# A fused transformer, minGRU, Runge-Kutta and expert kernel: another order of the fourth head's low parts, the last gates by k block, and most of the last drive's split moved into the first Runge-Kutta round

## What is computed

```
x = x + minGRU(adaLN_transformer(x, cond))        # 16 heads of 128, attention within a sequence; MLP 1024, gelu
x = x + top4_of_16_blocks_ffn(RK4(cond, cond, drive = x))

minGRU:  z = sigmoid(x Wz + bz);  n = g(x Wn + bn);  h_t = (1 - z_t) h_(t-1) + z_t n_t,  h_0 = 0.5
RK4:     per token step four stages of  dq = q - q^3/3 - p + drive + tanh(q) C^T + bias,  dp = 0.08 (q + 0.7 - 0.8 p)
ffn:     h = gelu(q W1^T), the 12 blocks of 64 columns with the smaller router logits set to 0;  y = h W2^T
```

## Time and profile before

| | us |
|---|---|
| median of 3 runs | 519.38 (519.37 to 520.13) |
| the profiled execution | 521.38 |
| its span | 519.5 |
| attention, four passes | to about 243 |
| MLP and gates | about 243 to 330 |
| Runge-Kutta scan | about 330 to 508 |

### The profile page before, as it was taken

How to read it: one execution, slowest core, us unless ns; L and a number is a source line. 1 busy time by engine, 2 the same in 40 slices (tenths; PEclk the granted TensorE clock), 3 DMA queues, 4 the chain that set the end, 5 groups by cost and what they waited for, 6 DMA issues and landing times.

```text
span 519.5 us, 13419 instructions
## 1 busy us (share of the span) xinstructions
PE 449.8 (87%) x4832; PEld 310.7 (60%) x4832; DVE 434.4 (84%) x1698; ACT 314.2 (60%) x872; POOL 48.4 (9%) x77
## 2 busy tenths in 40 slices
PE   2999989999999899997498996589797887888886
PEld 2655675557546665566244442478676776767676
DVE  4969876777776876979978776999999999999994
ACT  1378855786487748775467935464655646555563
POOL 2001320224021211042000000000000000000000
PEclk9899999999999999999789999596979879788899
DMA  8972402200202000000000000000000000000000
GB/s 292 415 305 62 105 4 78 61 21 0 81 21 61 0 1 0 0 1 0 0 1 1 0 1 0 3 2 0 2 1 11 11 0 11 1 11 11 1 10 22
DMA packets 10127, 20.82 MB, mean 40 GB/s; under 512 B 1456, under 2 KB 4720, under 8 KB 9456
## 3 DMA queue, kind: packets, MB, share of 16 engines
q1 hardware_dynamic: 9536, 19.89, 11.4%
q10 hardware_dynamic: 560, 0.60, 0.3%
HBM read 19.40 MB, written 1.08 MB: 39 GB/s over the span
## 4 chain that ended last, share of the span: by engine, by line
DVE 43%; PE 37%; ACT 10%; issue 5%; POOL 2%; DMA 2%; ACTq 0%; DVEq 0%
PE bank L765 33%; DVE base L1567 5%; DVE lin L1659 5%; DVE qs L1573 4%; DVE cub L1561 3%; DVE sq L1555 3%; ACT ptx L567 3%; PE score L765 3%; ACT ao_sb L535 2%; DVE pacc L1669 2%; POOL ptx L471 2%; ACT sraw L560 2%; PE spare L765 2%; DMA vec<-vecs 2%; DVE thlo L1551 1%
## 5 line engine op out<-in xcount | busy, mean ns | idle before, releaser
L765 PE MATMUL bank<-x,pairs_store 128*128 128x512 f16 x384 | 87.2, 384 | 0.0
L765 PE MATMUL score<-th,coup_part 128*128 128x32 f16 x1024 | 48.1, 182 | 19.4 <-ACT th L728 17.3
L765 PEld LDWEIGHTS bank<-x,pairs_store 128*128 128x128 f16 x384 | 37.7, 99 | 43.8 <-issue 2.2
L471 POOL TENSOR_TENSOR ptx<-pt,ptx 32x256 f16<-32x256 f32 x64 | 44.5, 696 | 190.8 <-ACT ptx L567 187.2
L535 ACT ACTIVATE big<-bank,pass_b 128x512 f16<-128x512 f32 x64 | 42.1, 683 | 23.5 <-DVE pass_b L1286 15.8
L728 ACT ACTIVATE th<-qs 128x64 f16<-128x64 f32 x96 | 24.4, 254 | 50.5 <-DVE qs L1573 50.5
L765 PEld LDWEIGHTS score<-th,coup_part 128*128 128x128 f16 x1024 | 36.4, 100 | 30.8 <-ACT th L728 29.3
L1298 DVE SCALAR_TENSOR_TENSOR big<-bank,pass_b,big 128x512 f16<-128x512 f32 x64 | 45.2, 739 | 7.5 <-ACT big L535 7.3
L765 PE MATMUL bank<-pairs_store,ao_sb 128*128 128x256 f16 x384 | 46.1, 273 | 5.2 <-DVE ao_sb L1298 1.9
L765 PEld LDWEIGHTS bank<-pairs_store,ao_sb 128*128 128x128 f16 x384 | 35.8, 98 | 12.7 <-DVE ao_sb L1298 4.3
L765 PE MATMUL bank<-pairs_store,x 128*128 128x512 f16 x192 | 43.4, 379 | 0.0
(11 more groups left out here) (197 smaller groups left out, 1017.9 us busy)
## 6 DMA issues: line engine op xcount, KB each, us to landing
wqk_sb<-wqk SPq DMA_DIRECT2D x16, 256.0 KB, 2.9
wv_sb<-wv SPq DMA_DIRECT2D x4, 512.0 KB, 5.7
wo_sb<-wo SPq DMA_DIRECT2D x4, 512.0 KB, 3.9
f_sb<-ffn_w SPq DMA_DIRECT2D x2, 1024.0 KB, 14.1
ao_sb<-xtok SPq DMA_DIRECT2D x4, 256.0 KB, 5.7
big<-ada_w SPq DMA_DIRECT2D x1, 1024.0 KB, 9.6
x_sb<-xT SPq DMA_DIRECT2D x1, 1024.0 KB, 13.4
w_sb<-w1T SPq DMA_DIRECT2D x1, 1024.0 KB, 16.2
```

The costliest lines, as they stand in the source:

```text
L471: nc.gpsimd.tensor_tensor(ptx[s, 1, :, s], pt[s], ptx[s, 0, :, s], ALU.subtract).then_inc(ptx_ready, 1)
L765: return nc.tensor.matmul(dst, lhsT, rhs, start=start, stop=stop, **kw)
```

## The change

*Attention, all passes.* VectorE: `low_projs(3)` and the first half of `low_pv(1)` go ahead of `normalise(2)`, the second half of `low_pv(1)` behind `shift(3)`, `normalise(3)` ahead of `add_heads(0, 0)`. ScalarE: three of the four copies of projection 3 ahead of `exps(2)` and the two strips of scores 3 ahead of `place_high(2)`. In all but the last pass `add_heads(1, 0)` goes ahead of `add_heads(0, 3)`.

*Gates.* For the second half and block 0 the products go by k block: both gates' k block 0 first, then k block 1; the first gate in two halves of 256 columns, one of them in `spare`. ScalarE and VectorE treat this piece in two halves. For the last piece ScalarE makes 1 - z (`za_last`) in VectorE's place.

*Drive split.* `drive_lows(0)` and `(1)` stand behind both scans of the first half. Of drives 2 and 3 VectorE makes the low part of the first four of 32 time steps ahead of the scan; the other 28 go in eight pieces of 7 time steps into the places of `split_h` in the first round. ScalarE makes the high part of drive 3 in two pieces (4 and 28 time steps), after the first two tanh of the scan.

*ScalarE's loop.* The two tanh stand at the end of a stage's work and wait for the next q; the first pair lies ahead of the loop, and one pair more runs at the end.

```diff
+        za_last = centred[:, 0]
...
@@ -609,12 +614,12 @@
                 empty_pv(0)
                 place_high(1)
                 copy_scores(2)
-                empty_projs(3, [0])
+                empty_projs(3, (0, 1, 2))
                 exps(2)
-                empty_projs(3, (1, 2, 3))
+                empty_projs(3, [3])
                 empty_pv(1)
+                copy_scores(3, NB4 // 2)
                 place_high(2)
-                copy_scores(3, NB4 // 2)
                 exps(3)
                 empty_pv(2)
                 place_high(3)
...
-            def drive_bias(n):
+            def drive_bias(n, used, times=slice(0, T)):
...
+                act.wait_ge(z_used, used)
+                nc.scalar.activation(drive_pair[:, 0, times, ob * B + h * nb:ob * B + (h + 1) * nb],
+                                     drive[:, ob, h * HALF:(h + 1) * HALF].rearrange("p (b t) -> p t b", t=T)[:, times],
                                      ACT.Identity, bias=c2_shifted[:, ob:ob + 1]).then_inc(drive_high, 1)
...
+            def relu_pair(n, piece, cols, ob, src, ready):
+
+                nc.scalar.activation(nneg_of[n % 2][:, cols], src[:, cols], ACT.Relu, bias=bn_neg[:, ob:ob + 1], scale=-1.0
+                                     ).then_inc(gate_in, 1)
+                nc.scalar.activation(nn_of[n % 2][:, cols], src[:, cols], ACT.Relu, bias=bn_twice[:, ob:ob + 1], scale=2.0
+                                     ).then_inc(ready, 1)
+                act.wait_ge(gate_in, piece + 1)
+                nc.scalar.activation(nneg_of[n % 2][:, cols], nneg_of[n % 2][:, cols], ACT.Tanh, scale=-0.5
+                                     ).then_inc(tn_ready, 1)
+
+            def gate_tanh(n, cols, ob, ready):
+
+                nc.scalar.activation(tz_of[n % 2][:, cols], bank[bank_of(USE_GRU[n // KB] + 2 * ob + 1)][:, cols], ACT.Tanh,
+                                     bias=hb[:, ob:ob + 1], scale=0.5).then_inc(ready, 1)
...
+            for ob in range(KB):
+                use = USE_GRU[0] + 2 * ob
+                wait_product(use)
+                relu_pair(ob, ob, every, ob, bank[bank_of(use)], free[bank_of(use)])
+                wait_product(use + 1)
+                gate_tanh(ob, every, ob, free[bank_of(use + 1)])
+            drive_bias(0, 1)
+            drive_bias(1, 2)
+
+            use = USE_GRU[1]
+            act.wait_ge(half_full, 1)
+            relu_pair(2, 2, first_half, 0, spare, half_ready)
+            wait_product(use + 1)
+            gate_tanh(2, first_half, 0, half_ready)
+            wait_product(use)
+            relu_pair(2, 3, second_half, 0, bank[bank_of(use)], free[bank_of(use)])
+            gate_tanh(2, second_half, 0, free[bank_of(use + 1)])
+            wait_product(use + 2)
+            relu_pair(3, 4, every, 1, bank[bank_of(use + 2)], free[bank_of(use + 2)])
+            wait_product(use + 3)
+            gate_tanh(3, every, 1, free[bank_of(use + 3)])
+            act.wait_ge(free[bank_of(use + 3)], count_of(use + 3) + 1)
+            nc.scalar.activation(za_last, tz_of[1], ACT.Identity, bias=one_half[:], scale=-0.5).then_inc(za_ready, 1)
+            drive_bias(2, 4)
+            act.wait_ge(q_ready, 1)
+            nc.scalar.activation(th16[:], qn[:].rearrange("p k b -> p (k b)"), ACT.Tanh).then_inc(th16_ready, 1)
+            nc.scalar.activation(th32[:], qn[:].rearrange("p k b -> p (k b)"), ACT.Tanh).then_inc(th32_ready, 1)
+            drive_bias(3, 5, slice(0, UNROLL))
+            drive_bias(3, 5, slice(UNROLL, T))
...
-                    act.wait_ge(q_ready, i * (4 * UNROLL) + n + 1)
-                    src = (qs[:, s - 1] if s else qn[:]).rearrange("p k b -> p (k b)")
-                    nc.scalar.activation(th16[:], src, ACT.Tanh).then_inc(th16_ready, 1)
-                    nc.scalar.activation(th32[:], src, ACT.Tanh).then_inc(th32_ready, 1)
...
+
+                    act.wait_ge(q_ready, i * (4 * UNROLL) + n + 2)
+                    src = (qs[:, s] if s < 3 else qn[:]).rearrange("p k b -> p (k b)")
+                    nc.scalar.activation(th16[:], src, ACT.Tanh).then_inc(th16_ready, 1)
+                    nc.scalar.activation(th32[:], src, ACT.Tanh).then_inc(th32_ready, 1)
...
+            def last_gates():
+
+                dst = [fill(USE_GRU[1] + w) for w in range(2)]
+                middle = HALF // 2
+                wn_half = (spare[:, 0:middle], dst[0][:, middle:HALF])
+
+                def gate(k, c):
+                    return mm(wn_half[c], wn_sb[:, k, 0:P], x3[:, k, HALF + c * middle:HALF + (c + 1) * middle], k == 0, k == KB - 1)
+
+                pe.wait_ge(x3_ready, KB + 1)
+                for c in range(2):
+                    gate(0, c)
+                mm(dst[1][:], wz_sb[:, 0, 0:P], x3[:, 0, HALF:N], True, False)
+                pe.wait_ge(x3_ready, 2 * KB)
+                gate(1, 0).then_inc(half_full, 1)
+                mm(dst[1][:], wz_sb[:, 1, 0:P], x3[:, 1, HALF:N], False, True).then_inc(full[bank_of(USE_GRU[1] + 1)], 1)
+                gate(1, 1).then_inc(full[bank_of(USE_GRU[1])], 1)
+                for w, weights in enumerate((wn_sb, wz_sb)):
+                    product(USE_GRU[1] + 2 + w, lambda k: weights[:, k, P:2 * P], lambda k: x3[:, k, HALF:N], KB)
...
-            gates(1)
+            last_gates()
...
                 shift(2)
+                low_projs(3)
+                low_pv(1, [0])
                 normalise(2)
-                low_projs(3)
-                low_pv(1)
                 last_strips()
                 shift(3)
+                low_pv(1, [1])
+                normalise(3)
                 add_heads(0, 0)
-                normalise(3)
                 low_pv(2, [0])
                 add_heads(0, 1)
                 low_pv(2, [1])
                 add_heads(0, 2)
                 if i < NQUAD - 1:
                     low_pv(3)
-                    add_heads(0, 3)
                     for c in range(KB * NH):
                         add_heads(1, c)
+                        if c == 0:
+                            add_heads(0, 3)
                         low_weights(i + 1, c)
                 else:
                     close_heads(0)
...
+            def min_gru(n, piece, cols, nn_in, tz_in, za_in=None):
+
+                h, ob = n // KB, n % KB
+                a = za[:, cols] if za_in is None else za_last
+                at = slice(h * HALF + cols.start, h * HALF + cols.stop)
+                twice, four = npos[:, cols], zb[:, cols]
+                dve.wait_ge(tn_ready, piece + 1)
+                dve.wait_ge(*nn_in)
+                own.step(V.scalar_tensor_tensor(twice, nneg_of[n % 2][:, cols], 1.0, nn_of[n % 2][:, cols], ALU.add, ALU.add))
+                dve.wait_ge(*tz_in)
+                if za_in is None:
+                    own.step(V.tensor_scalar(a, tz_of[n % 2][:, cols], -0.5, 0.5, ALU.mult, ALU.add))
+                own.wait()
+                own.step(V.scalar_tensor_tensor(four, tz_of[n % 2][:, cols], 1.0, twice, ALU.add, ALU.mult))
+                if za_in is not None:
+                    dve.wait_ge(*za_in)
+                own.wait()
+
+                a0, b0 = tok(a)[:, :, 0:1], tok(four)[:, :, 0:1]
+                own.step(V.scalar_tensor_tensor(b0, a0, 2.0, b0, ALU.mult, ALU.add))
+                own.wait()
+                own.step(V.memset(a0, 0.0))
+                own.wait()
+                own.step(V.tensor_tensor_scan(twice, a, four, 0.0, ALU.mult, ALU.add))
+                own.wait()
+                V.scalar_tensor_tensor(drive[:, ob, at], twice, 0.25, x_sb[:, ob, at], ALU.mult, ALU.add
+                                       ).then_inc(z_used, 1)
...
+            def drive_lows(n, highs, times=slice(0, T), done=drive_low):
...
+                dve.wait_ge(drive_high, highs)
+                ins = V.scalar_tensor_tensor(drive_pair[:, 1, times, at],
+                                             drive[:, ob, h * HALF:(h + 1) * HALF].rearrange("p (b t) -> p t b", t=T)[:, times],
+                                             c2_shifted[:, ob:ob + 1], drive_pair[:, 0, times, at], ALU.add, ALU.subtract)
+                if done is not None:
+                    ins.then_inc(done, 1)
...
-            min_gru(0)
+            every, first_half, second_half = slice(0, HALF), slice(0, HALF // 2), slice(HALF // 2, HALF)
+            for n in range(KB):
+                use = USE_GRU[0] + 2 * n
+                min_gru(n, n, every, emptied(use), emptied(use + 1))
+                dve.wait_ge(z_used, n + 1)
+            drive_lows(0, 1)
+            drive_lows(1, 2)
             residual(1)
             V.tensor_copy(qn[:], cond_sb[:]).then_inc(q_ready, 1)
-            min_gru(1)
+            use = USE_GRU[1]
+            min_gru(2, 2, first_half, (half_ready, 1), (half_ready, 2))
+            dve.wait_ge(z_used, 3)
+            min_gru(2, 3, second_half, emptied(use), emptied(use + 1))
+            dve.wait_ge(z_used, 4)
```

(15 more changed lines are left out.)

63 lines of the change are left out of this document (11 added, 52 removed).

## The result

The changed kernel took 517.25 us (median; 515.88 to 518.83) beside 521.21 us (519.37 to 523.41) for the kernel before: ratio 0.9924, 95% interval 0.9904 to 0.9944, so 3.96 us less (interval 2.9 to 5.0), where 3.7 less was forecast. In a second comparison it took 518.97 beside 521.32: ratio 0.9954, interval 0.9939 to 0.997, so 2.35 less (1.6 to 3.2), which leaves 3.7 out. The profiled execution took 517.7 us, its span 515.9. Five launches of 587 to 2171 us, in two of the five comparisons, are left out of all whole times. The distances up to the first q repeat within 0.05 us from one execution to the next, the scan within 0.22.

The account below looks back on a forecast made before the run. Bounds: a latency loop in the 128 Runge-Kutta stages; before them, waits in attention tails, last gates and last drive's split. Sum: -0.84 + 0.77 - 4.10 + 0.2 + 0.3 = -3.7, from 519.38 to 515.7 us; range 514.1 to 517.9.

Parts of the forecast that it names:

- Order on VectorE: Attention pass tail: with the new order place_high(3) no longer waits for the probabilities, gaining 0.21 us a pass, 0.84 in four.
- rival 1: Attention tail and round edges: VectorE work beside GpSimd and dearer edges take back 1.1 us, giving 518.1; chance 0.13.
- Swap: Three attention passes: add_heads(1,0) ahead of add_heads(0,3) delays out_project(1,3), costing 0.26 us a pass, 0.77 in three.
- Part A: Attention tail, new order and exchanged additions together: -0.1 us, bounds -1.5 and +0.5.
- Last drive: Last gates and minGRU ahead of the scan: last drive at 325.10 instead of 327.34, 2.24 us earlier.
- First q: Start of the Runge-Kutta stages: first q 4.10 us earlier, bounds 3.3 and 4.4, limited by ScalarE's scale and following low work.
- Low parts in round 1: First round of stages: pieces of the drive splits replace split_h, costing 0.2 us, bounds 0 and 0.7.
- Round edges: Seven round edges: ScalarE's loop jump, no longer hidden, costs 0.04 us each, 0.3 in all, bounds 0 and 7 x 0.2.
- Rival 3: Seven round edges: ScalarE's jump waits in the open for an instruction fetch, 15.4 us lost, giving 530.8; chance 0.04.
- Part B: From the last gates to the first stage: reordered gates and shorter drive splits gain 4.10 us, bounds 3.3 and 4.4.
- Rival 4: Last gates: they don't start early, so nothing is left of the 2.24 us, giving 517.9; chance 0.09.
- Rival 2: Attention passes: exchanging the two additions gains 0.23 us instead of costing 0.26, add_heads(1,1) being early enough, giving 514.2; chance 0.12.

Follow-up runs that it names:

- the repeats: The kernel before and the changed kernel, each run and profiled again unaltered: 522.79 us and 518.97 us.
- tanh_first: Changed kernel with the tanh pair back at the head of each stage of ScalarE's loop, none ahead of it: ratio 0.9949 to the kernel before.
- adds_tanh_first: Changed kernel with add_heads(1,0), (1,1), (0,3) ahead of the next quad's first low_weights, and tanh at each stage's head: 518.52 us, ratio 0.9945.

## Why the prediction was right

The time saved was 3.96 in one comparison, close to the forecast of 3.7, and 2.35 in the other, whose interval leaves 3.7 out. The absolute forecast of 515.7 started from 519.38, a low median; beside 521.21 the changed kernel took 517.25. Inside the traces, from the project(0) that starts pass 2 to the last q, the two pairs give -3.57 (before and after: 428.82 to 425.25) and -3.91 (the repeats: 428.98 to 425.07).

- *Order on VectorE*: forecast -0.21 a pass, measured -0.15. The mechanism is as written, place_high(3) without a wait. GpSimd's run for the third head grew from 2.88 to 2.95, and with it the path to mix(2), so that empty_pv(2) starts 0.04 later in the pass than before, not 0.05 earlier; this is rival 1's collision at a fifth of its price. VectorE's shift beside that run took 0.80, where it took 0.64. The Trainium skill (SBUF — State Buffer, Who interferes with whom) says that a VectorE operation with two SBUF inputs and a GpSimd operation that reads SBUF exclude each other for their whole length: VectorE's 0.80 agrees, but in GpSimd's 2.95 against 2.88, the same in every trace with the new order, the other side pays 0.07 in this run and no more.
- *Swap*: forecast +0.26, measured +0.18. The second wait came as predicted. Counted from the start of the 24 matmuls, the bank was full at 2.34, add_heads(1, 0) began at 2.37 (forecast 2.38) and out_project(1,2) at 3.21 (3.22); add_heads(1, 1) ended at 4.86 (4.87). The mis-sized term is the last one: out_project(1,3) began 0.06 after that release, at 4.92, where the forecast took over the 0.15 of the first release and had 5.02. (VectorE's 0.26 of idle time against 0.36 in the forecast changes nothing: the forecast counted from 130.52, where the next record already overlaps the end of low_pv(3).) Part A: -0.15 x 4 + 0.18 x 3 = -0.06, forecast -0.1.
- *Last drive*: forecast -2.24, measured -2.05. The two halves took 2.69 and 2.65 (forecast 2.65), the whole last one 3.91 (319.67 to 323.58), not 3.80, and the first began 0.06 late.
- *First q*: forecast -4.10, measured -3.66, inside its bounds. Beside the 0.19 of the drive, the queue behind ScalarE's scale was mis-sized, and it is this path that ended last. The first scaled copy was done 1.52 after the last drive, where the forecast has 1.40 (326.5 - 325.10). From there to q it took 0.61 and not 0.45: the prediction put one piece of the low work beside `base`, but there are two (48 columns at 325.14, 64 at 325.48). The splits of 64 columns ahead of the scan missed too, 0.31 and 0.32 instead of 0.22, but TensorE's path had 0.09 to spare. Their price was taken from a 64-column operation that reads in order; the split reads with a stride, and its own rows ((1.07 - 0.16)/512 a column plus 0.16) would have given 0.27.
- *Low parts in round 1*: forecast 0.2, measured 0.60 in stages 1 to 14, and 0.08 more in stage 0, just inside the bound of 0.7. The prices were close (0.40 for 0.37); the step that failed is "a stage has 0.08 to 0.2 of slack at that place". In stages 10 to 14 it has none.
- *Round edges*: forecast 0.3. The seven edges together take 10.32 us after, against 10.07 before; but the repeat has 10.08 against 10.05, tanh_first has 10.10, and adds_tanh_first, whose jump is the old one too, 10.26. So the new place of the jump costs 0 to 0.25 in all and can't be told from nothing. The edge of the earlier trace rows, 1.53, is the longest of the seven in that trace; the others take 1.41 to 1.44. Rival 3, which wanted 0.57 an edge, is refuted.
- *Not in the forecast*: the waits at instruction loads. Rounds 2 to 8 without their edges take 145.55 before (145.67 in the repeat) and 145.06 after (145.07), and the 1.60 us stage 1 of before is gone. The loop's new order isn't the cause: tanh_first, with the old one, takes 145.15. These 0.7 us paid for the low parts.

So the mechanisms were right, but that the sum came so close is partly luck, because sizes missed in opposite senses: Part B ahead of the scan brought 0.44 less than forecast, the pieces in round 1 cost 0.5 more, and the edges and the instruction loads, the latter not foreseen at all, gave some 0.9 back. Rival 4 is refuted: the k-block order alone is worth 0.78 at the last drive. Rival 2 is refuted for this order and true for another.

## What to carry to other kernels

When an add is moved ahead to free one buffer, look at the second buffer that the same consumer needs: freeing the first 0.24 earlier cost 0.18 a pass, because it held up the second; freeing both early won 0.24. Price a small piece of an operation from its own larger form (start plus width), not from another operation of the same width, and look for slack in each stage that takes a piece, not in a typical one. Where edits are worth under a microsecond in 500, judge them by distances between landmarks in the trace.
